# Mean product and cond's product in four column strips of TensorE's array

## The reference

```python
hidden = concatenate([cond, cond], axis=-1)                   # (4, 512)
x_mean = mean(x, axis=1, keepdims=True)                       # (4, 1, 512)
fused = concatenate([x, x_mean * ones_L, hidden[:, None, :] * ones_L], axis=-1)
relation = relu(einsum('bld,do->blo', fused, W) + b)
return x + relation
```

## Time and profile before

| | |
|---|---|
| median of 3 runs | 119.92 us (119.19 to 120.28) |
| span of the profiled execution | 117.4 us |
| TensorE matmul (PE) busy | 103.1 us, 88% |
| VectorE (DVE) busy | 87.0 us, 74% |
| ScalarE (ACT) busy | 48.2 us, 41% |
| GpSimd (POOL) busy | 46.7 us, 40% |
| mean granted TensorE clock | 0.958 |

### The profile page before, as it was taken

How to read it: one execution, slowest core, us unless ns; L and a number is a source line. 1 busy time by engine, 2 the same in 40 slices (tenths; PEclk the granted TensorE clock), 3 DMA queues, 4 the chain that set the end, 5 groups by cost and what they waited for, 6 DMA issues and landing times.

```text
span 117.4 us, 1775 instructions
## 1 busy us (share of the span) xinstructions
PE 103.1 (88%) x490; PEld 82.0 (70%) x490; DVE 87.0 (74%) x163; ACT 48.2 (41%) x118; POOL 46.7 (40%) x46
## 2 busy tenths in 40 slices
PE   5919999935999879997999999999999999999910
PEld 2309998812478568875888888778888886999900
DVE  1028859860289799999999995499999996897640
ACT  4057516700105988006848700077495001833310
POOL 6358310034000000089785840046856339992000
PEclk9995999999599999999999999999999999999995
DMA  2999999999999999990785809400076292295986
GB/s 89 258 228 229 220 212 232 380 240 223 222 224 221 224 220 221 220 167 4 163 197 127 236 12 233 113 0 0 0 170 188 51 248 58 62 241 135 253 219 170
DMA packets 35975, 20.28 MB, mean 173 GB/s; under 512 B 1920, under 2 KB 34688, under 8 KB 35968
## 3 DMA queue, kind: packets, MB, share of 16 engines
q1 hardware_dynamic: 34528, 18.88, 74.5%
q10 hardware_dynamic: 1248, 0.79, 2.5%
q0 software_dynamic: 192, 0.52, 1.8%
HBM read 11.80 MB, written 8.39 MB: 172 GB/s over the span
## 4 chain that ended last, share of the span: by engine, by line
PE 49%; SPq 23%; DMA 10%; DVE 9%; issue 3%; ACT 2%; ACTq 0%
PE ps_y L410 47%; SPq L162 15%; DMA xa<-in_x_dram 10%; SPq L141 3%; DVE back L317 2%; SPq L171 2%; DVE w2x L334 2%; DVE ps_xt L300 2%; PE ps_mean L428 1%; ACT xh L236 1%; DVE xl L306 1%; ACT relu_t L256 1%; DVE bias_row L348 1%; SPq L169 1%; SPq L173 1%
## 5 line engine op out<-in xcount | busy, mean ns | idle before, releaser
L410 PE MATMUL ps_y<-xh,w1h 128*128 128x256 f32 (+2 forms) x160 | 55.1, 370 | 4.3 <-ACT xh L236 2.4
L206 POOL TENSOR_TENSOR xa<-xa,back 128x512 f32 x28 | 36.0, 1304 | 42.8 <-DVE back L317 42.8
L410 PE MATMUL ps_y<-xl,w1h 128*128 128x256 f32 (+2 forms) x160 | 52.3, 353 | 0.0
L410 PE MATMUL ps_y<-xh,w1l 128*128 (+2 forms) x144 | 50.3, 366 | 0.0
L410 PEld LDWEIGHTS ps_y<-xh,w1h 128*128 128x128 f32 x160 | 29.5, 197 | 11.0 <-issue 4.4
L256 ACT ACTIVATE relu_t<-ps_y,bias 128x512 f32<-128x512 f32 (+1 forms) x32 | 19.9, 633 | 33.0 <-DVE bias L351 25.6
L410 PEld LDWEIGHTS ps_y<-xl,w1h 128*128 128x128 f32 x160 | 29.5, 196 | 4.8 <-issue 1.2
L300 DVE STREAM_TRANSPOSE ps_xt<-xa 128x512 f32<-128x512 f32 (+1 forms) x36 | 22.2, 641 | 13.5 <-DMA xa<-in_x_dram 13.2
L236 ACT ACTIVATE xh<-ps_xt 128x512 fp32r<-128x512 f32 (+1 forms) x36 | 19.7, 549 | 26.2 <-DVE ps_xt L300 25.9
L410 PEld LDWEIGHTS ps_y<-xh,w1l 128*128 128x128 f32 x144 | 27.1, 189 | 4.5
L306 DVE TENSOR_TENSOR xl<-ps_xt,xh 128x512 fp32r<-128x512 f32 (+1 forms) x36 | 22.2, 618 | 4.2 <-ACT xh L236 4.2
(11 more groups left out here) (21 smaller groups left out, 22.1 us busy)
## 6 DMA issues: line engine op xcount, KB each, us to landing
xa<-in_x_dram SPq DMA_DIRECT2D x28, 256.0 KB, 6.5
out_dram<-xa SPq DMA_DIRECT2D x28, 256.0 KB, 3.8
xa<-in_x_dram SPq DMA_DIRECT2D x8, 128.0 KB, 5.9
w<-in_L_cond_W_dram SPq DMA_DIRECT2D x4, 256.0 KB, 6.8
w<-in_L_cond_W_dram SPq DMA_DIRECT2D x2, 512.0 KB, 9.7
w<-in_L_cond_W_dram POOLq DMA_DIRECT2D x4, 128.0 KB, 4.7
out_dram<-xa SPq DMA_DIRECT2D x4, 128.0 KB, 2.7
out_dram<-xa ACTq DMA_DIRECT2D x4, 128.0 KB, 2.4
```

Of the source, the lines that this page charges most:

```text
L206: nc.gpsimd.tensor_tensor(rows, rows, back[:, t], ALU.add).then_inc(added, 1)
L410: return nc.tensor.matmul(ps_y[:, t, ls], lhs, rhs, start=start, stop=stop, skip_group_check=True)
```

## The change

Cond's product and the mean product are no longer computed as one product with 128 columns of weights and 512 of moving data. Each becomes four products, one for each strip j of 32 columns of TensorE's array, whose result lands on partitions 32j to 32j+31, with 128 columns of moving data, the columns 128j to 128j+127. The results have the form 128x128 that bias_row needs. VectorE makes const_row and bias_row in one operation of 128x128 each. The matrix of ones and the spread condition shrink to 32 columns, so that GpSimd makes one copy of the condition instead of four. b is loaded in four transfers of 128 numbers to 32 partitions each, instead of 512 numbers to 128 partitions.

```diff
-        ones = sb("ones", [P, P])
+        ones = sb("ones", [P, Q])
-        cond_t = sb("cond_t", [P, CK, NQ, Q])
-        b_row = sb("b_row", [P, D])
+        cond_t = sb("cond_t", [P, CK, Q])
+        b_row = sb("b_row", [P, P])
-        ps_const = psum("ps_const", [P, D])
-        ps_mean = psum("ps_mean", [P, D])
+        ps_const = psum("ps_const", [P, NL])
+        ps_mean = psum("ps_mean", [P, NL])
@@ sync
-            sp.dma_start(b_row[:], bvec.partition_broadcast(P)).then_inc(b_landed, 16)
+            for j in range(NQ):
+                sp.dma_start(b_row[Q * j:Q * j + Q], bvec[P * j:P * j + P].partition_broadcast(Q)).then_inc(b_landed, 16)
@@ gpsimd
-            for j in range(NQ):
-                nc.gpsimd.tensor_copy(cond_t[:, :, j, 0:B], cond_c[:].rearrange("p b k -> p k b")).then_inc(cond_spread, 1)
+            nc.gpsimd.tensor_copy(cond_t[:, :, 0:B], cond_c[:].rearrange("p b k -> p k b")).then_inc(cond_spread, 1)
@@ vector, sum_bias
-                for j in range(NQ):
-                    rows, cols = slice(Q * j, Q * j + Q), slice(P * j, P * j + P)
-                    nc.vector.scalar_tensor_tensor(out=bias_row[rows], in0=ps_mean[rows, cols], scalar=1.0 / L, in1=const_row[rows],
-                                                   op0=ALU.mult, op1=ALU.add).then_inc(bias_summed, 1)
-                dve.wait_ge(bias_summed, NQ * (b + 1))
+                nc.vector.scalar_tensor_tensor(out=bias_row[:], in0=ps_mean[:, 0:P], scalar=1.0 / L, in1=const_row[:],
+                                               op0=ALU.mult, op1=ALU.add).then_inc(bias_summed, 1)
+                dve.wait_ge(bias_summed, b + 1)
@@ vector
-            for j in range(NQ):
-                rows, cols = slice(Q * j, Q * j + Q), slice(P * j, P * j + P)
-                nc.vector.tensor_tensor(const_row[rows], ps_const[rows, cols], b_row[rows, cols], ALU.add).then_inc(const_ready, 1)
-            dve.wait_ge(const_ready, NQ)
+            nc.vector.tensor_tensor(const_row[:], ps_const[:, 0:P], b_row[:], ALU.add).then_inc(const_ready, 1)
+            dve.wait_ge(const_ready, 1)
@@ tensor, mean_bias
-                nc.tensor.matmul(ps_mean[:], ones[:], w2x[:], start=True, stop=True).then_inc(mean_done, 1)
+                for j in range(NQ):
+                    last = nc.tensor.matmul(ps_mean[Q * j:Q * j + Q, 0:P], ones[:, 0:Q], w2x[:, P * j:P * j + P], start=True, stop=True)
+                last.then_inc(mean_done, 1)
@@ tensor, after tile 0 of group 1
-                    for k in range(CK):
-                        last = nc.tensor.matmul(ps_const[:], cond_t[:, k].rearrange("p j b -> p (j b)"), w3sum[:, k],
-                                                start=(k == 0), stop=(k == CK - 1))
+                    for j in range(NQ):
+                        for k in range(CK):
+                            last = nc.tensor.matmul(ps_const[Q * j:Q * j + Q, 0:P], cond_t[:, k], w3sum[:, k, P * j:P * j + P],
+                                                    start=(k == 0), stop=(k == CK - 1))
```

More of the change, by code:

```diff
@@ L372, in _ @@
             dve.wait_ge(const_summed, 1)
-            dve.wait_ge(b_landed, 16)
-            for j in range(NQ):
-                rows, cols = slice(Q * j, Q * j + Q), slice(P * j, P * j + P)
-                nc.vector.tensor_tensor(const_row[rows], ps_const[rows, cols], b_row[rows, cols], ALU.add).then_inc(const_ready, 1)
-            dve.wait_ge(const_ready, NQ)
+            dve.wait_ge(b_landed, 16 * NQ)
+            nc.vector.tensor_tensor(const_row[:], ps_const[:, 0:P], b_row[:], ALU.add).then_inc(const_ready, 1)
+            dve.wait_ge(const_ready, 1)
             sum_bias(0)
@@ L453, in _ @@
                 if t == 0:
-                    pe.wait_ge(cond_spread, NQ)
+                    pe.wait_ge(cond_spread, 1)
                     pe.wait_ge(w3_added, 1)
-                    for k in range(CK):
-                        last = nc.tensor.matmul(ps_const[:], cond_t[:, k].rearrange("p j b -> p (j b)"), w3sum[:, k],
-                                                start=(k == 0), stop=(k == CK - 1))
+                    for j in range(NQ):
+                        for k in range(CK):
+                            last = nc.tensor.matmul(ps_const[Q * j:Q * j + Q, 0:P], cond_t[:, k], w3sum[:, k, P * j:P * j + P],
+                                                    start=(k == 0), stop=(k == CK - 1))
                     last.then_inc(const_summed, 1)
```

## The result

The changed kernel takes 114.66 us (median of 4 runs, 114.40 to 114.98), beside 119.56 us for the kernel before: a ratio of 0.959, with a 95% interval of 0.953 to 0.965. The span of the profiled execution fell from 117.4 to 112.9 us, by 4.5.

The account below looks back on a forecast made before the run. TensorE was taken to bound the kernel; 2.30 us of its waits closing plus 0.3 from its own products made 2.6, off the 119.92 us median: 117.3 us. The range was 115.0 to 118.9 us.

Parts of the forecast that it names:

- The bound and the holes: TensorE from 31 us to the end: the one bound, with 2.30 us of holes (1.34 + 0.89 + 0.07) that close.
- A: Rival, chance 0.12: all four strips run side by side, 5.0 us saved, 114.9; sign: TensorE waiting for VectorE near 39 and 51 us.
- VectorE's price: Const and bias on VectorE: a 128x128 operation takes 0.31 us, so the first place gives 1.92, each later bias 0.93.
- b's load: Broadcast of b shrinks from 256 KB to 64 KB, so VectorE's wait for group 2 gets 0.89 us shorter.
- TensorE's own products: Strip products on TensorE, only neighbours overlapping: +0.06 us a mean product, -0.5 the first block, -0.3 in all.
- the sign of being right: On TensorE, the mean product between two ordinary tiles takes 0.7 to 1.1 us.
- going over and back: TensorE switching to strips and back, a drain each way: 0.32 us a product, 0.64 at half clock.
- The second gap: TensorE's wait for ScalarE's group 2 eviction, 53.66 to 54.55: 0.89 us, forecast to close with 1.1 to spare.
- B: Rival, chance 0.16: strips cost more than they save, no overlap, drains and fixed cost 1.9 us on TensorE; 119.5 us.
- C: Rival, chance 0.06: TensorE's clock stays at half for 3.4 us more, past 32.4, losing 1.7; 119.0 us.
- D: Rival, chance 0.06: short passes no longer cover weight loads, up to 0.225 us more on each of 48; 128.4 us.
- The range: Measured time between 115.0 and 118.9 us, with less than 2 in 10 outside.

Follow-up runs that it names:

- the moved product: Changed kernel with cond's and the first mean product behind tile 2 of group 1 on TensorE instead of tile 0: 116.96 us, ratio 0.973.

## Why the prediction was off

**The bound and the holes: right.** The kernel was bound by TensorE with two waits for ScalarE, and behind both stood VectorE's strip-wise operations. VectorE's part alone closed both gaps and took 2.7 off the span, for 2.30 forecast. In the whole change short waits came back at the same places, 0.50 idle before 39.13 and 0.22 before 50.97: TensorE had become faster than VectorE there, which was named as the sign of A.

**VectorE's price: right.** 0.28 to 0.29 us for 128x128; from const to the next turning 33.25 - 32.38 = 0.87 us in place of 35.88 - 33.10 = 2.78, so 1.91 shorter for 1.92 forecast.

**b's load: likely right in sign, unsettled in size.** 0.72 for 0.89, within the scatter of executions.

**TensorE's own products: wrong, and this is the step that failed.** It says that "in-order work can lay the last pass of a strip beside the first of the next and no more". I took the order of the code for the order of the array. Four strips ran at once in either order. From that step came +0.06 for a mean product, which measured -0.31 (0.57 against 0.88, below the 0.7 to 1.1 named as the sign of being right), and -0.5 for the first block, which measured -2.5 (4.1 to 1.62 us): -0.3 in all against -3.4. The other two prices in that step were good: 0.32 for going over and back measured 0.36, and 0.108 for a round measured 0.107. With 0.36 + 2 x 0.107 for a mean product the sum comes out without any new term.

**Where the surplus went.** Of the first block's 2.5 not all could be had: TensorE was then ready for group 2 at 38.47, before the eviction ended at 38.83, and waited 0.50. Group 2 started 2.63 sooner, for 1.34 + 0.5 forecast. Three mean products gave 0.9, where I had counted a loss of 0.2. The second gap closed by 0.67 of its 0.89: the last pass of group 2 starts at 50.52 and the next at 50.97. And 0.3 came from the break at 77 us in the kernel before, two passes that start at 77.11 and 77.50, for which 0.07 was counted; why it is absent after is not known. Together that is 4.5 us of span for 2.6 forecast. The rest of the miss in time is in the medians: the forecast started from 119.92, and with a fourth run the kernel before stands at 119.56. The prediction puts 2.5 us around the span; in every run on record it is about 1.8, so the profiled execution was the one of 119.19 and not the median. The sum does not use this term.

**The rival that came true was A**, at a chance of 0.12. Its places were met: group 2 at 39.13 for 38.95, group 3 at 50.97 for 50.9. Its prices were not: it saved 0.65 a mean product and 3.1 in the first block, with nothing for going over and back, where 0.31 and 2.5 were measured. So its 5.0 us of span were 4.5, and that its 114.9 lies so near 114.66 is in part luck. It was left at a low chance because of that same sentence about order, although the packing rule of the Trainium skill (TensorE: Matmul & The Clock Gate, Measured speedup vs the span model) stood beside it. With that rule's form, one pass plus a few nanoseconds for each further tile, the traces agree: four passes start within 0.04 us, and a round of four takes 0.107, as one pass does. The drain rule of the Trainium skill (TensorEngine Tiling (Array Packing), Key Properties) is in accord with the fixed 0.36, which the run with fourfold products splits off; that this is a drain is inferred and not shown.

**B, C and D.** D is out: loads of weights cost nothing beyond a round of 0.107. B's cost of going over and back is real (0.36), but its lack of overlap is not. C, a longer half clock, did not come in the profile after. It did come in the runs with the four operations and with the moved product, which were slower than their sums, and in those with the strips alone, with b's load alone and with the strips in the inner loop.

**The range** ended at A's own time, 115.0 for 114.9, as if that case had no spread. A case that is taken in should be taken in with its own error.

## What to carry to other kernels

Price small products in column strips as one fixed cost for the detour (0.36 us here) plus the number of rounds of four, not by the order in which they are written. Look for the gain of a shorter operation at the wait behind it: here one VectorE operation in place of four was worth more (about 3.7 us) than the strips that made it possible (1.5 to 2.1), and the strips by themselves gave only about 0.5 as long as VectorE was late. And before idle time of TensorE is moved, look at what runs behind it: the half clock that follows costs nothing where there is slack and full price where there is none.

## What the runs showed that was not expected

32 short passes with their loads of weights take 32 / 4 x 0.107 us, so on average a pass with its load is issued each 0.027 us. A pass of 128 columns in one strip alone takes 0.109, a quarter of a whole pass of 512, so the strip costs nothing by itself.

A TensorE made faster ahead of a wait can bring a dearer wait. With the strips alone it stood idle for 4.37 us instead of 1.18, and the clock was 0.50 for the 6 us that followed:

```profile
40.80:46.80 6.00, 5.94 (x14) 4.69 (x15) 5.52 (x10) 4.35 (x11) 0.00 (x0) 0.50 1.21 230
```

Two things made this wait. The strips ended group 1 sooner, and cond's product also started at 26.42 instead of 27.87, as w3sum was ready sooner in that execution. The run with b's load alone, with whole products and cond's at 25.69, waited 3.36 us at the same place, and the clock was 0.61 from 40.0 to 44.4. So the wait belongs to group 2's late eviction, and not to the strips alone. With the strips alone TensorE then started group 3 itself, at 55.27 instead of 54.55, without a gap; the kernel kept its time because the mean products and the break at 77 us gave that back.
